# VectorE's small instructions before the first tokens: one operand each moved from SBUF to PSUM

## The reference

```python
x = x + _L0_conv_ref(_gn(x), ...)      # inside _L0_conv_ref:
    u = jnp.stack([mean, mx, std], axis=-1)
    med = jnp.median(u.reshape(b, -1), axis=-1)[:, None, None]
    u = (u - med) ** 3
    z = jnp.einsum('bck,ck->bc', u, cfc_w)
    g = jax.nn.sigmoid(z / jnp.sqrt(1.0 + BN_EPS) * bn_w + bn_b)
    return x * g[:, :, None, None]
t = _to_tokens(x)
t = t + _L1_attn_ref(_ln_t(t), w_q, w_k, w_v, w_o)   # windowed, 16 heads, tanh softcap
t = t + _L1_ffn_ref(_ln_t(t), ...)                   # top 2 of 8 experts, and a shared expert
```

## Time and profile before

| | us |
|---|---|
| median of 3 runs (lowest, highest) | 807.95 (807.74, 811.38) |
| profiled execution: first to last instruction | 807.8 |
| VectorE busy / TensorE busy, whole span | 418.2 / 674.9 |
| end of the statistics and the gate, start of L990 | 91.22 |

### The profile page before, as it was taken

The page is one execution under the profiler, slowest core; times in us unless marked ns, Lnnn a source line. Parts: engine busy times, 40 slices in busy tenths (PEclk is TensorE's granted clock), DMA queues, the critical chain, the costliest instruction groups (busy, mean ns, idle before and its releaser), DMA issues.

```text
span 807.8 us, 13633 instructions
## 1 busy us (share of the span) xinstructions
PE 674.9 (84%) x4859; PEld 540.8 (67%) x4860; DVE 418.2 (52%) x1022; ACT 269.8 (33%) x462; POOL 278.9 (35%) x324
## 2 busy tenths in 40 slices
PE   0001299989898989899988999999979999999991
PEld 0000287878786868686867889999856667766760
DVE  7898534464644454455425489722354444444441
ACT  7330116262625353535345222343511111111110
POOL 1770002232323132322223111376635555455531
PEclk9999999999997999798999999999999999999997
DMA  8540000010101010100101453334275555555543
GB/s 287 155 131 0 0 1 2 1 54 1 52 0 52 0 52 0 52 0 31 49 27 54 154 199 105 105 105 159 74 249 100 102 101 102 102 103 104 104 67 39
DMA packets 24786, 62.08 MB, mean 77 GB/s; under 512 B 3056, under 2 KB 7152, under 8 KB 23728
## 3 DMA queue, kind: packets, MB, share of 16 engines
q1 hardware_dynamic: 15344, 41.16, 14.8%
q0 software_dynamic: 8736, 20.45, 14.2%
q10 hardware_dynamic: 672, 0.03, 0.1%
HBM read 38.56 MB, written 23.07 MB: 76 GB/s over the span
## 4 chain that ended last, share of the span: by engine, by line
PE 43%; DMA 24%; issue 13%; DVE 12%; ACT 4%; POOL 3%; SPq 0%; DVEq 0%; POOLq 0%; ACTq 0%
DMA out_tokens<-yo,dest 23%; PE PS L1349 15%; PE scores L1349 11%; PE scores L1576 5%; PE PS L1444 5%; PE scores L1430 3%; ACT probs L640 2%; DVE v L867 2%; POOL probs L491 1%; PE PS L1399 1%; POOL att_l L497 1%; DVE col L882 1%; DMA T<-in_x 1%; DVE col L878 1%; DVE qT L807 1%
## 5 line engine op out<-in xcount | busy, mean ns | idle before, releaser
L1349 PE MATMUL scores<-xb,sw 128*128 128x256 f32 x768 | 97.6, 283 | 0.0
L1349 PEld LDWEIGHTS scores<-xb,sw 128*128 128x128 f32 x768 | 95.1, 191 | 2.1 <-issue 0.4
L566 POOL DMA_INDIRECT out_tokens<-yo,dest x39 | 61.8, 1584 | 93.3 <-DMA out_tokens<-yo,dest 91.1
L491 POOL TENSOR_SCALAR_AFFINE_SELECT probs<-probs 128x256 f32<-128x256 f32 x128 | 51.5, 429 | 110.3 <-ACT probs L644 109.5
L1349 PE MATMUL PS<-xt_h,w_h 128*128 128x256 f32 x256 | 77.6, 303 | 1.5 <-DVE xt_l L1020 1.5
L640 ACT ACTIVATE probs<-scores 128x768 f32<-128x768 f32 x64 | 51.5, 804 | 74.7 <-PE scores L1430 74.7
L1657 PE MATMUL scores<-wd_sb,ehT 128*128 x156 | 73.5, 593 | 1.0 <-DVE ehT L1309 1.0
L1349 PE MATMUL PS<-xt_l,w_h 128*128 128x256 f32 x256 | 74.3, 290 | 0.0
L1349 PE MATMUL PS<-xt_h,w_l 128*128 128x256 f32 x256 | 73.9, 289 | 0.0
L1035 DVE RECIPROCAL rden<-PS 128x256 f32<-128x256 f32 x32 | 56.3, 1758 | 31.6 <-PE PS L1444 31.5
L758 ACT ACTIVATE es<-scores 128x256 f32<-128x256 f32 x39 | 15.0, 384 | 161.7 <-PE scores L1349 161.7
(11 more groups left out here) (255 smaller groups left out, 1390.6 us busy)
## 6 DMA issues: line engine op xcount, KB each, us to landing
wgu_l<-in_wgu SPq DMA_DIRECT2D x8, 1024.0 KB, 6.8
T<-in_x SPq DMA_DIRECT2D x8, 512.0 KB, 8.4
probs<-in_wqkvo SPq DMA_DIRECT2D x8, 512.0 KB, 4.2
x_rows<-x SPq DMA_DIRECT2D x8, 512.0 KB, 2.8
x_cols<-x2T SPq DMA_DIRECT2D x8, 512.0 KB, 2.6
xc<-x_cols SPq DMA_DIRECT2D x8, 512.0 KB, 3.4
out_tokens<-T SPq DMA_DIRECT2D x8, 512.0 KB, 7.5
wd_sb<-in_wd SPq DMA_DIRECT2D x8, 512.0 KB, 6.7
```

The costliest lines, as they stand in the source:

```text
L491: ins = pool.affine_select(out=t, in_=t, compare_op=ALU.is_ge, fill=0.0, base=0, pattern=[[0, 2], [1, P]], channel_multiplier=-1)
L566: pool.indirect_dma_start(out[:, :], bass.IndirectOffsetOnAxis(dest[:, t:t + 1], 0), yo[:, t % 3, :], None, compute_op=ALU.add).then_inc(y ...
L1349: ins = pe.matmul(out, lhs(k, a), rhs(k, b), start=m == 0, stop=m == len(products) - 1)
```

## The change

VectorE's small instructions of the statistics and of the search get one operand in PSUM where both tensors lay in SBUF. The matrix `uT` is no longer copied out of `PS[2]` but read there. `width` and `fourths` of the search lie in `PS[7]`, the statistics' vectors in `PS[6]`. No changed two-input instruction has both inputs in PSUM, so some values are kept twice, once in either memory (`small[:, 1]` and `mean_gap`, `K(7)` and `dev`), and two sums become reductions. ScalarE writes the squares' sums into `PS[6]` and makes the mean of its images itself (one more instruction); VectorE now waits for all of ScalarE's sums ahead of its first small instruction.

```diff
@@ -198,11 +198,8 @@
         small = kf[:, 0:16 * n32].rearrange("p (k n) -> p k n", n=n32)
         var2 = kf[:, 16 * n32:18 * n32]
         root = kf[:, 18 * n32:20 * n32]
-        root2 = kf[:, 20 * n32:22 * n32]
-        inv2 = kf[:, 22 * n32:24 * n32]
         u = vf[:, 0:B * UP]
         uw = vf[:, B * UP:4 * B * UP].rearrange("p (k n) -> p k n", k=3)
-        uT = vf[0:B * UP, 4 * B * UP:4 * B * UP + P]
         junk = vf[0:B * UP, 4 * B * UP + P:4 * B * UP + 4 * P].rearrange("p (k n) -> p k n", k=3)
         counted = vf[0:B * UP, 4 * B * UP + 4 * P:4 * B * UP + 4 * P + 2].bitcast(bf16)[:, 0:3]
@@ -275,6 +272,14 @@
         gu_bank, dn_bank = PS[0:2], PS[2:4]
         route_bank, ids_bank = PS[4], PS[5]
         egu_bank, ey_bank, xT_bank, hT_bank = PS[0], PS[2], PS[6], PS[7]
+        search = PS[7][0:B * UP, 0:6]
+        uT = PS[2][0:B * UP, 0:P]
+        by_channel = PS[6].rearrange("p (k n) -> p k n", n=B * CB)
+        mean_sum, mean_gap, gap_square, m2_all, dev, top_dev, r_half = (by_channel[:, k, :] for k in range(7))
+        inv2, root2 = PS[6][:, 8 * B * CB:10 * B * CB], PS[6][:, 10 * B * CB:12 * B * CB]
         def sem(name):
@@ -596,11 +601,12 @@
                                      accum_out=small[:, 12, c:c + 1])
             ins.then_inc(act_sums, 1)
             act.wait_ge(act_sums, 1)
+            act.activation(small[:, 3, 0:na], small[:, 12, 0:na], ACT.Copy, scale=1.0 / S)
             act.activation(small[:, 13, 0:na], small[:, 12, 0:na], ACT.Copy, scale=-1.0 / S).then_inc(act_sums, 1)
             act.wait_ge(act_sums, 2)
             for b, k, c in cols:
                 ins = act.activation(unread[c], at(T, b)[:, k * S:(k + 1) * S], ACT.Square,
-                                     bias=small[:, 13, c:c + 1], accum_out=small[:, 5, c:c + 1])
+                                     bias=small[:, 13, c:c + 1], accum_out=m2_all[:, c:c + 1])
             ins.then_inc(act_sums, 1)
             for k in range(NW):
@@ -780,7 +786,7 @@
             fill(powers[:, :], -0.5)
             fill(gate_sb[:, :, :], 0.0)
             below, lo, lo_part = col[:, 0:1], col[:, 1:2], col[:, 2:3]
-            thr, base, width, fourths = col[:, 3:6], col[:, 6:9], col[:, 11:14], col[:, 14:17]
+            thr, base, width, fourths = col[:, 3:6], col[:, 6:9], search[:, 0:3], search[:, 3:6]
             cnt, flags = col[:, CNT:CNT + 3], col[:, 20:23]
             for j in range(3):
                 fill(thr[:, j:j + 1], -RANGE / 2 + (j + 1) * RANGE / 4)
@@ -818,46 +824,47 @@
             na = CB * ACT_STATS
-            kb = [small[:, k, na:n32] for k in range(6)]
             mean_of, m2_of = bst[:, na:n32, 1:5:3], bst[:, na:n32, 2:6:3]
-            step_of(dve.tensor_tensor(kb[0], mean_of[:, :, 0], mean_of[:, :, 1], ALU.add))
-            step_of(dve.tensor_tensor(kb[1], mean_of[:, :, 0], mean_of[:, :, 1], ALU.subtract))
-            dve.wait_ge(dve_step, step_of(dve.tensor_tensor(kb[2], m2_of[:, :, 0], m2_of[:, :, 1], ALU.add)))
-            dve.wait_ge(act_sums, 2)
-            step_of(dve.tensor_scalar(small[:, 3, 0:na], small[:, 13, 0:na], -1.0, None, ALU.mult))
-            dve.tensor_scalar(kb[3], kb[0], 0.5, None, ALU.mult).then_inc(chmean_ready, 1)
-            dve.wait_ge(dve_step, step_of(dve.tensor_tensor(kb[4], kb[1], kb[1], ALU.mult)))
+            dve.wait_ge(act_sums, 3)
+            step_of(dve.tensor_reduce(small[:, 2, na:n32], m2_of, AX.X, ALU.add))
+            dve.wait_ge(dve_step, step_of(dve.tensor_reduce(mean_sum[:, na:n32], mean_of, AX.X, ALU.add)))
+            dve.tensor_scalar(small[:, 3, na:n32], mean_sum[:, na:n32], 0.5, None, ALU.mult).then_inc(chmean_ready, 1)
+            step_of(dve.scalar_tensor_tensor(small[:, 1, na:n32], mean_of[:, :, 0], 2.0, mean_sum[:, na:n32],
+                                             ALU.mult, ALU.subtract))
             dve.wait_ge(dve_step, step_of(dve.scalar_tensor_tensor(
-                kb[5], kb[4], S / 4.0, kb[2], ALU.mult, ALU.add)))
-            dve.wait_ge(act_sums, 3)
+                mean_gap[:, na:n32], mean_of[:, :, 0], 2.0, mean_sum[:, na:n32], ALU.mult, ALU.subtract)))
+            dve.wait_ge(dve_step, step_of(dve.tensor_tensor(
+                gap_square[:, na:n32], mean_gap[:, na:n32], small[:, 1, na:n32], ALU.mult)))
+            dve.wait_ge(dve_step, step_of(dve.scalar_tensor_tensor(
+                m2_all[:, na:n32], gap_square[:, na:n32], S / 4.0, small[:, 2, na:n32], ALU.mult, ALU.add)))
             dve.wait_ge(grpmean_ready, 1)
             grp_mean = K(6)
-            dve.wait_ge(dve_step, step_of(dve.tensor_copy(grp_mean, PS[0][:, 0:n32])))
-            dve.wait_ge(dve_step, step_of(dve.tensor_tensor(K(7), K(3), grp_mean, ALU.subtract)))
-            dve.wait_ge(dve_step, step_of(dve.tensor_tensor(K(8), K(7), K(7), ALU.mult)))
-            dve.scalar_tensor_tensor(K(9), K(5), 1.0 / S, K(8), ALU.mult, ALU.add).then_inc(chvar_ready, 1)
-            step_of(dve.tensor_scalar(var2[:, n32:2 * n32], K(5), 1.0 / (S - 1), 1e-30, ALU.mult, ALU.max))
+            step_of(dve.tensor_tensor(dev, K(3), PS[0][:, 0:n32], ALU.subtract))
+            dve.wait_ge(dve_step, step_of(dve.tensor_tensor(K(7), K(3), PS[0][:, 0:n32], ALU.subtract)))
+            dve.wait_ge(dve_step, step_of(dve.tensor_tensor(K(8), dev, K(7), ALU.mult)))
+            dve.scalar_tensor_tensor(K(9), m2_all, 1.0 / S, K(8), ALU.mult, ALU.add).then_inc(chvar_ready, 1)
+            step_of(dve.tensor_scalar(var2[:, n32:2 * n32], m2_all, 1.0 / (S - 1), 1e-30, ALU.mult, ALU.max))
             dve.wait_ge(grpvar_ready, 1)
             dve.tensor_scalar(var2[:, 0:n32], PS[1][:, 0:n32], EPS, None, ALU.add).then_inc(var_ready, 1)
-            step_of(dve.tensor_tensor(K(10), chmax, grp_mean, ALU.subtract))
+            step_of(dve.tensor_copy(grp_mean, PS[0][:, 0:n32]))
+            step_of(dve.tensor_tensor(top_dev, chmax, PS[0][:, 0:n32], ALU.subtract))
             dve.wait_ge(root_ready, 1)
             dve.wait_ge(dve_step, step_of(dve.reciprocal(inv2, root)))
-            dve.wait_ge(dve_step, step_of(dve.tensor_tensor(root2, var2, inv2, ALU.mult)))
+            dve.wait_ge(dve_step, step_of(dve.tensor_tensor(root2, inv2, var2, ALU.mult)))
             dve.wait_ge(dve_step, step_of(dve.tensor_tensor(root2, root2, root, ALU.add)))
-            dve.wait_ge(dve_step, step_of(dve.reciprocal(inv2[:, 0:n32], root2[:, 0:n32])))
-            r = inv2[:, n32:2 * n32]
-            dve.wait_ge(dve_step, step_of(dve.tensor_scalar(r, inv2[:, 0:n32], 2.0, None, ALU.mult)))
+            dve.wait_ge(dve_step, step_of(dve.reciprocal(r_half, root2[:, 0:n32])))
+            r = K(10)
+            dve.wait_ge(dve_step, step_of(dve.tensor_scalar(r, r_half, 2.0, None, ALU.mult)))
             u3 = u.rearrange("p (n k) -> p n k", k=UK)
-            dve.tensor_tensor(u3[:, :, 0], K(7), r, ALU.mult)
-            dve.tensor_tensor(u3[:, :, 1], K(10), r, ALU.mult)
+            dve.tensor_tensor(u3[:, :, 0], dev, r, ALU.mult)
+            dve.tensor_tensor(u3[:, :, 1], top_dev, r, ALU.mult)
             dve.scalar_tensor_tensor(u3[:, :, 2], root2[:, n32:2 * n32], 0.5, r, ALU.mult, ALU.mult).then_inc(u_ready, 1)
             dve.wait_ge(uT_full, 1)
-            dve.wait_ge(dve_step, step_of(dve.tensor_copy(uT, PS[2][0:B * UP, 0:P])))
@@ -879,7 +886,7 @@
                     thr, width, below, base, ALU.mult, ALU.add)))
             def new_base():
-                dve.wait_ge(dve_step, step_of(dve.tensor_scalar(col[:, 11:17], col[:, 11:17], 0.25, None, ALU.mult)))
+                dve.wait_ge(dve_step, step_of(dve.tensor_scalar(search, search, 0.25, None, ALU.mult)))
                 dve.wait_ge(dve_step, step_of(dve.tensor_scalar(base, fourths, thr[:, 0:1], None, ALU.add)))
             def narrow(i):
```

## The result

The changed kernel takes 789.05 us (median of four runs, 783.72 to 790.73), the kernel before 808.03 (four runs, 807.74 to 811.38). Ratios here are taken over the runs within 1.5% of their kernel's fastest: this one is 0.9729, with a 95% interval of 0.9672 to 0.9785, where the quotient of the two medians is 0.9765. The profiled execution of the changed kernel took 790.58 us, 1.78 more than its span of 788.8.

The account below looks back on a forecast made before the run. VectorE's own chain to the first image's gate was taken as the bound. Gains of 21.3 us less 1.5, 0.2 and 0.7 gave 18.9 us, a span of 788.9 and a median of 789.0, range 785.0 to 793.5.

Parts of the forecast that it names:

- What bounds the stage, and the cause: Ahead of the first image's gate: VectorE is itself the chain; its small all-SBUF instructions wait until GpSimd's running instruction ends.
- one shared path: Statistics and search: one access path to SBUF, shared by some VectorE forms with GpSimd, free when GpSimd's instruction ends.
- The stalls: Waits on GpSimd that the change removes: 8.8 us ahead of the search, 12.0 us in its 16 rounds.
- What stayed exposed: Subtraction between the seventh and eighth search rounds, still all in SBUF: waits 1.5 us for GpSimd, bounds nothing to 2.3.
- PSUM's price: Operands in PSUM on the chain: small reads nothing, three instructions on 128 columns 0.2 us, awaited writes 0.7 us.
- The term for writes: VectorE's awaited PSUM writes on the chain: 0.03 us each, 0.7 us in all, bounds nothing to 4.4.
- the 23: VectorE's awaited PSUM writes on the chain: six in the statistics, 16 widths, one subtraction.
- The 0.2 forecast: Three instructions on 128 columns lose a faster read from SBUF: 0.2 us for the three.
- operands in PSUM are dear: Rival: some 119 chain instructions each lose 0.06 us, 7.1 in place of 0.7, giving 795.4 us; chance 0.11.
- The rest moves as a whole: Behind the gate nothing else is late; the same work moves as a whole with the stage's 18.9 us.
- The clock: Rival: TensorE's clock falls elsewhere, 3.9 us a fall; one more 792.9 (chance 0.15), one fewer 785.1 (0.10).
- the count mostly stays: Whole kernel: the number of TensorE clock falls mostly stays, as two of three runs and the profile lie within 0.2 us.

## Why the prediction was right

**What bounds the stage, and the cause.** Right, and shown: where GpSimd's reading is taken away (only writes), the two-input stalls go with VectorE untouched; where its instruction is cut to a quarter, the stalls shrink to a third; where VectorE's operand moves to PSUM, they go. The first reading was too coarse in two points. I named one shared path, and there are two ways to collide. And I took all small instructions with their tensors in SBUF to be held up, but for the counts; the form decides there too. The trace of before already had a reciprocal that ran freely inside the subtraction from 29.99, in the 352 ns of the like one far behind GpSimd's last (L978):

```profile
30.11 0.35 DVE L850 RECIPROCAL kT<-kT 128x32 f32<-128x32 f32 x1
```

The reduction L829 of after is another such form, so the saving ahead of the search is not all due to PSUM.

**The stalls.** Ahead of the search 8.8 + 0.5 us were forecast, 9.21 measured; in the rounds 12.0 forecast, 11.77 measured. These are right for this execution, with the reservation of the experiments: before, the statistics' loss is a matter of phase (one more instruction was hit when only the search was changed), and the two parts do not add up if only one of them is done.

**What stayed exposed.** 1.5 us forecast; 1.39 lost in that stretch in all, of which 1.33 are the instruction's own and 0.07 those of L911, now in PSUM. It came at 42.39 and not 43.0, and GpSimd's subtraction ran from 41.52 to 43.92 and not from 42.3 to 44.6; both were early by about as much.

**PSUM's price.** The term for writes, 0.7 us, was too large. A product of 64 columns that writes PSUM takes 233 ns, against 224 and 225 for the two in SBUF before; the width, L889, takes 164, as L882 of before does once GpSimd is done (59 to 91 us). Sixteen of the 23 are widths, and the statistics' writes took 4 to 15 ns longer than in SBUF, so that the 23 cost some 0.1 us. Reading costs 5 ns a count. The 0.2 forecast for the three `tensor_scalar` instructions on 128 columns came true: L911 took 354 ns where L904 of before took 281, and the two that find the middle numbers 346 (L925) where they took 282 (L918). The stretch behind the exposed instruction, which holds those two, lost 0.18 us. The rival "operands in PSUM are dear" falls with that. By the Trainium skill, "VectorE: DVE Perf Modes", section "The TRN2 errata — SBUF-src ops pay a fixed extra latency per instruction", an operand in PSUM would cost 62 cycles more, an estimate of 65 ns at the page's 0.96 GHz. The runs agree for the three on 128 columns alone (64 to 73 ns), not for the counts (5 ns) or the small instructions (15 at most).

**The rest moves as a whole.** The stage gained 19.75 us for a forecast 18.9. Of the 0.85 difference, 0.34 lies ahead of the first small instruction, whose start varies from 21.98 to 22.59 over the nine executions whatever the kernel, and most of the remainder is the price of writes.

**The clock.** This step failed, though the number hides it: that the profile stood for the median run, and that the count of falls mostly stays. I took the profiled span to lie 0.15 us below the median. The changed kernel's execution takes 1.8 us more than its span, so the profile of before, at some 809.6 us by that, was not the median run but probably one with a lower clock. The forecast, the median less 18.9, does not move by that; the trust in the count does. And "the count mostly stays" was read from three runs: 24 later runs of the kernel before spread from 803.33 to 816.70. The rest after the affine takes 714.1 us at a mean clock of 0.977 and 723.7 at 0.961, with one and the same work. The medians of the changed kernel happened to hold about as many falls as those of before, so 789.05 meets 789.0 more closely than the working deserves; the range, which had room for one fall either way, is what the working supports. At a mean clock of 0.961 to 0.963 the kernels took 796.92 and 815.25 to 816.70, at 0.978 they took 785.41 and 807.25: 18 to 22 us apart, which fits the 19.75 of the stage.

What decides in which step TensorE's clock falls, and why more falls come in one execution than in another, was not tried.

## What to carry to other kernels

Small VectorE instructions whose tensors all lie in SBUF should be read against GpSimd's timeline: if their ends coincide with the ends of GpSimd's instructions, the chain pays for whole GpSimd instructions. One operand in PSUM, an accumulator that nobody needs, or shorter GpSimd instructions are three ways out, and the first two cost no more than 15 ns for a small instruction here (73 for one on 128 columns in PSUM), while the third brought the affine to 84.47 only. When only part of such a chain is freed, count again how long the other part now runs beside GpSimd; and judge a gain of a few microseconds by the start of the next stage, not by the whole time, when runs of one and the same kernel lie up to 13 us apart, with their mean clock.

## What the runs showed of the hardware

- A GpSimd subtraction of 128x1024 cut into quarters took 2.7 us (38.4 / 14) instead of 2.35.
- A two-input VectorE instruction in SBUF ran at 0.20 us beside a GpSimd fill, and at up to 2.39 beside a GpSimd subtraction.
- A VectorE `tensor_scalar` of 96x6 in SBUF beside a GpSimd subtraction took 1.55 us, and 0.21 when it also wrote an accumulator. A reciprocal (0.35) and a reduction (0.21) in SBUF were not held up either.
- A `tensor_scalar` of 96x6 in SBUF took up to 0.99 us beside a GpSimd fill of 0.95.
- A VectorE instruction that writes PSUM took as long as in SBUF at 6 columns (164 ns) and 4 to 15 ns longer at 20 to 64. A `tensor_scalar` on 128 columns took 281 to 282 ns with its tensors in SBUF, 346 reading PSUM and 354 with both in PSUM.
- The same work behind the affine takes between 714 and 724 us by the mean granted clock, 0.977 to 0.961.
